# The low part of a pair's queries in six banks behind the last six blocks of key features

## What is computed

```python
q, k, v = heads(xn @ Wq), heads(xn @ Wk), heads(xn @ Wv)        # 16 heads of 64, 1250 rows
q_prime = relu(q @ proj)                                         # proj is 64 x 256
k_prime = relu(k @ proj)
kv   = einsum('bhsf,bhsd->bhfd', k_prime, v)
attn = einsum('bhsf,bhfd->bhsd', q_prime, kv)
norm = einsum('bhsf,bhf->bhs', q_prime, k_prime.sum(axis=2))
attn = attn / (norm + EPS);  mix = attn @ Wo + bo
```

## Time and profile before

| | |
|---|---|
| median of 3 runs | 1439.13 us (1438.02 to 1443.07) |
| the profiled execution | 1438.47 us |
| its span, first to last instruction | 1436.8 us |
| PE busy | 1378.5 us (96%), 7434 matmuls |
| weight loads (PEld) busy | 1261.5 us (88%) |
| DVE busy | 876.0 us (61%) |
| ACT busy | 534.5 us (37%) |
| POOL busy | 171.3 us (12%) |
| mean granted clock of PE | 0.991 |

### The profile page before, as it was taken

The page is one execution under the profiler, slowest core; times in us unless marked ns, Lnnn a source line. Parts: engine busy times, 40 slices in busy tenths (PEclk is TensorE's granted clock), DMA queues, the critical chain, the costliest instruction groups (busy, mean ns, idle before and its releaser), DMA issues.

```text
span 1436.8 us, 19199 instructions
## 1 busy us (share of the span) xinstructions
PE 1378.5 (96%) x7434; PEld 1261.5 (88%) x7434; DVE 876.0 (61%) x1604; ACT 534.5 (37%) x629; POOL 171.3 (12%) x169
## 2 busy tenths in 40 slices
PE   6999999999999999899999999999999989999995
PEld 5888889999999999899999999999978868888884
DVE  6555668787887787645766522445566785544423
ACT  4333244444453543414222223432211225554533
POOL 0011211101101001000000000000000343322212
PEclk9999999999999999999999999999999989999998
DMA  9765432432432433948454014222185665988764
GB/s 311 234 170 128 89 54 32 101 79 36 91 88 34 85 73 56 349 127 220 128 143 120 20 55 127 84 86 69 59 219 172 165 223 158 294 224 232 197 175 73
DMA packets 108573, 193.22 MB, mean 134 GB/s; under 512 B 32289, under 2 KB 77337, under 8 KB 106764
## 3 DMA queue, kind: packets, MB, share of 16 engines
q1 hardware_dynamic: 88563, 145.83, 34.5%
q0 software_dynamic: 19920, 46.17, 16.3%
HBM read 129.38 MB, written 72.21 MB: 140 GB/s over the span
## 4 chain that ended last, share of the span: by engine, by line
PE 71%; DMA 14%; DVE 7%; ACT 3%; issue 2%; SPq 1%; POOLq 0%; ACTq 0%; DVEq 0%
PE slot L2153 23%; PE slot L2311 13%; DMA adj_d<-stage 8%; PE slot L2381 5%; PE slot L2204 5%; PE slot L2212 5%; PE lsb L2212 4%; PE slot L2109 3%; PE kvb L2345 3%; PE slot L2095 2%; PE slot L2084 2%; DMA adj_d<-eye_dram 2%; PE slot L2190 1%; DMA mix_d<-mixn 1%; DMA dx<-x_dram 1%
## 5 line engine op out<-in xcount | busy, mean ns | idle before, releaser
L2153 PE MATMUL slot<-big_hi,slab_h 128*128 128x418 f32 x768 | 193.9, 360 | 9.5 <-DVE qp_l L1755 4.8
L2153 PE MATMUL slot<-big_lo,slab_h 128*128 128x418 f32 x768 | 188.7, 354 | 0.0
L2153 PE MATMUL slot<-big_hi,slab_l 128*128 128x418 f32 x768 | 187.9, 353 | 0.0
L2153 PEld LDWEIGHTS slot<-big_hi,slab_h 128*128 128x128 f32 x768 | 139.2, 189 | 14.4 <-DVE qp_l L1755 6.4
L2153 PEld LDWEIGHTS slot<-big_hi,slab_l 128*128 128x128 f32 x768 | 144.8, 189 | 2.3
L2153 PEld LDWEIGHTS slot<-big_lo,slab_h 128*128 128x128 f32 x768 | 144.7, 189 | 2.1
L1000 POOL DMA_DIRECT2D adj_d<-stage x80 | 67.1, 839 | 483.1 <-ACT stage L1120 364.7
L1393 DVE TENSOR_TENSOR big_lo<-slot,big_hi 128x1024 fp32r<-128x1024 f32 (+2 forms) x70 | 63.2, 928 | 100.2 <-ACT big_hi L1120 100.0
L2311 PE MATMUL slot<-adj,xs_h 125*128 125x418 f32 x480 | 118.1, 354 | 0.5 <-DVE ztmp L1393 0.5
L2311 PE MATMUL slot<-adj,xs_l 125*128 125x418 f32 x480 | 117.4, 353 | 0.0
L1397 DVE TENSOR_SCALAR oh_src<-lane,src_lo 125x125 bf16<-125x125 f16 x320 | 84.0, 263 | 25.5 <-PE kvb L1969 18.3
(11 more groups left out here) (360 smaller groups left out, 2855.2 us busy)
## 6 DMA issues: line engine op xcount, KB each, us to landing
slab_raw<-slabs_dram SPq DMA_DIRECT2D x40, 512.0 KB, 4.2
adj_d<-stage POOLq DMA_DIRECT2D x81, 117.2 KB, 3.1
plain_l<-w_dram SPq DMA_DIRECT2D x16, 512.0 KB, 7.3
w_home<-w_dram SPq DMA_DIRECT2D x8, 1024.0 KB, 5.9
plain_h<-w_dram SPq DMA_DIRECT2D x14, 512.0 KB, 6.2
adj_d<-eye_dram POOLq DMA_DIRECT2D x1, 6250.0 KB, 25.3
raw<-adj_d SPq DMA_DIRECT2D x3, 1828.8 KB
dx<-x_dram SPq DMA_DIRECT2D x10, 448.0 KB
```

Of the source, the lines that this page charges most:

```text
L2153: mm = ten.matmul(ps[:, 512 * q:512 * q + CW], w[a][:, kt, :], big[b][:, kt, CW * q:CW * q + CW], start=(kt == 0 and c == 0), stop=(kt == ...
```

## The change

In ORDER a step QL is put behind each of KK 4 to KK 9, six to a pair: QL (p, h, q) is the low part of bank q (418 columns) of half h, with h = (i - 4) // 3 and q = (i - 4) % 3. The step QE stays where it was, but only ACT (high part) and SP act on it; in `DVE_KINDS` QL stands in its place. So the low part of half 0 is made in three subtractions of 64 x 418 behind the low parts of KK 4, 5 and 6, that of half 1 in three behind KK 7, 8 and 9, where one subtraction of 64 x 1254 stood behind KK 4 and one behind KK 7. The waits of PE name the last bank of the half: `free_slot` behind Q waits for ("QL", p, 1, 2), `feature_product` of half 0, block 0 for ("QL", p, 0, 2). Each QL waits for ACT's QE of its half and increments dve_done.

```diff
--- before.py
+++ after.py
@@ -145,6 +145,7 @@
             o += [("EP", last), ("E", last)]
         for i in range(3, NT):
             o += [("KV", p, i - 3), ("KK", p, i)] + {4: [("QE", p, 0)], 7: [("QE", p, 1)]}.get(i, [])
+            o += [("QL", p, (i - 4) // 3, (i - 4) % 3)] if i >= 4 else []
         if not more:
             o += [("KV", p, NT - 3), ("KV", p, NT - 2), ("RH", p - 1), ("QP", p, 0, 0), ("KV", p, NT - 1), ("KC", p),
                   ("QP", p, 0, 1), ("S", p)]
@@ -219,7 +220,7 @@
 PSUM_KINDS = {"DG", "DT", "Z", "H", "HT", "XT", "V", "K", "Q", "KK", "QP", "AT",
               "O", "OT", "N", "FT", "R", "RT", "PX"}
 ACT_KINDS = PSUM_KINDS - {"OT", "PX", "DG", "DT", "Q", "N"} | {"P", "ZP", "KC", "S", "RH", "LNB", "MP", "RP", "QE", "WV", "VL"}
-DVE_KINDS = {"ZP", "Z", "P", "XT", "WV", "VL", "K", "QE", "KK", "S", "QP", "RC", "RH", "OT", "N", "DN", "DT",
+DVE_KINDS = {"ZP", "Z", "P", "XT", "WV", "VL", "K", "QL", "KK", "S", "QP", "RC", "RH", "OT", "N", "DN", "DT",
              "FL", "FT", "RK", "RX", "SL", "MP", "RP"}
 
 
@@ -1725,14 +1726,18 @@
                     dve.wait_ge(act_done, ACTED[k])
                     tt(v_cols(v_p[1][:, :, :]), v_cols(v_raw[:, :, :]),
                        v_cols(v_p[0][:, :, :].bitcast(F32)), ALU.subtract).then_inc(dve_done, 1)
-                elif kind in ("K", "QE"):
-                    parts = k_s if kind == "K" else q_s
-                    ps = sums[SLOT[(kind[0], k[1])]]
-                    for h in (0, 1) if kind == "K" else k[2:]:
-                        dve.wait_ge(*((half_made, k[1] + 1) if kind == "K" and h == 0 else (act_done, ACTED[k])))
-                        ins = tt(chunks(parts[h][own[1 - h], :]), cols(ps)[own[h]],
-                                 chunks(parts[h][own[h], :].bitcast(F32)), ALU.subtract)
+                elif kind == "K":
+                    for h in range(2):
+                        dve.wait_ge(*((half_made, k[1] + 1) if h == 0 else (act_done, ACTED[k])))
+                        ins = tt(chunks(k_s[h][own[1 - h], :]), cols(ps)[own[h]],
+                                 chunks(k_s[h][own[h], :].bitcast(F32)), ALU.subtract)
                     ins.then_inc(dve_done, 1)
+                elif kind == "QL":
+                    p, h, q = k[1:]
+                    part = slice(CW * q, CW * q + CW)
+                    dve.wait_ge(act_done, ACTED[("QE", p, h)])
+                    tt(q_s[h][own[1 - h], part], sums[SLOT[("Q", p)]][own[h], 512 * q:512 * q + CW],
+                       q_s[h][own[h], part].bitcast(F32), ALU.subtract).then_inc(dve_done, 1)
                 elif kind == "KK":
                     dve.wait_ge(act_done, ACTED[k])
                     dve.scalar_tensor_tensor(
@@ -1946,7 +1951,7 @@
                     elif before[0] == "DG":
                         ten.wait_ge(deg_ready, 1)
                     elif before[0] == "Q":
-                        ten.wait_ge(dve_done, DVED[("QE", before[1], 1)])
+                        ten.wait_ge(dve_done, DVED[("QL", before[1], 1, 2)])
                     elif before[0] == "AT" and before[2] == 0:
                         ten.wait_ge(act_done, ACTED[before])
                         ten.wait_ge(nrm_low, before[1] + 1)
@@ -2089,7 +2094,7 @@
 
                 p, h, f = k[1:]
                 if h == 0 and f == 0:
-                    ten.wait_ge(dve_done, DVED[("QE", p, 0)])
+                    ten.wait_ge(dve_done, DVED[("QL", p, 0, 2)])
                 for c, part in enumerate((proj_h, proj_l[h])):
                     for q in range(3):
                         mm = ten.matmul(ps[:, 512 * q:512 * q + CW], part[:, 128 * f:128 * f + 128],
```

## The result

The changed kernel takes 1455.31 us (median of 4 runs, 1454.67 to 1458.65), the kernel before 1440.05 us (median of 4, 1438.02 to 1443.07): the ratio is 1.0108, with a 95% interval of 1.0092 to 1.0125. It is 15.3 us slower; 13.0 was forecast. The profiled execution took 1458.65 us, the slowest of the four; its span is 1457.0 us. One execution of experiment 4 took 1528.23 us at a mean granted clock of 0.848 and is left out of that experiment's median and ratio.

A forecast was written before the change was run, and what follows sets the result against it. PE was taken to bound the kernel (71% of the chain of waits), delayed by DVE. Seven pairs at +1.82 us plus 0.3 for the last gave +13.0: 1452.1 us median, 1451.5 profiled; range 1446.0 to 1456.5.

The forecast's parts named there:

- The place of the cost: On PE, QP of half 0, block 0 waits for q's last bank, with KV 8, KV 9 and the next K slab queued behind.
- Duration of a bank, 0.59: On DVE, each 64 x 418 subtraction takes 0.59 us, from a straight line between measured shapes; ends 0.43 and 0.68.
- No overlap around a bank: On DVE, a bank and a neighbouring low part of KK don't overlap: 0.62 and 0.70 us, a round of 1.32.
- rival (a): DVE's rounds are shorter, with overlap ahead of a bank: +1.38 us a pair, 1449.1 us in all; chance 0.18.
- A pair, 1.82: In pairs 0 to 6, PE's first QP starts 1.82 us later per pair, the removed KV 5 stall of 0.59 included.
- The last pair, +0.3: In the last pair, the store of att is issued up to 0.5 us later behind DVE; 0.3 us counted.
- rival (d): PE's new wait of 2.4 us at QP lowers its clock: 17 us more, 1469 us; chance 0.03.
- a granted clock under 1.00 between 185 and 620 us: Sign of a wrong prediction: PE's clock falls below its upper level, 2.4 GHz, in the stretch of the head pairs.
- the priced 2.4: Cost per pair if PE ran at half clock behind its QP wait for a stretch as long as the wait: 2.4 us.
- The sum: Seven pairs at 1.82 us and 0.3 for the last: 13.0 us slower, profile 1451.5, median 1452.1 us; chance 0.66.
- The range: Total time from 1446.0 to 1456.5 us; the long end, 2.36 us a pair, gives 1456.1, plus 0.4 for spread.
- banks of 0.68 us: Long end of a bank's duration on DVE, from the 512 row; without overlap +2.36 us a pair.

The follow-up runs named there:

- experiment 4: Changed kernel with QP of half 0, block 0 moved behind KV 8, KV 9 and KC in pairs 0 to 6: 1445.16 us, ratio 1.0028 to before.
- Experiments 3: Changed kernel without the subtraction of bank 2 of half 1 in pairs 1 to 7, QP waiting for bank 1: 1448.56 us, ratio 1.004 to before.
- experiment 1: Changed kernel with its six bank subtractions at the old places, three behind KK 4 and three behind KK 7: 1441.29 us, ratio 0.9999 to before.
- experiment 5: Changed kernel run again: 1457.14 us, ratio 1.0102 to before; with ten added matmuls in PE's wait at QP in pairs 0 to 6: 1452.03 us.
- experiment 6: Changed kernel with the six banks two row blocks earlier, behind the low parts of KK 2 to KK 7: 1437.87 us, ratio 0.9965 to before.

## Why the prediction was right, and where its sizes were off

- *The place of the cost.* That QP waits for the last bank, and that KV 8, KV 9 and the K slab stand behind it, is what the trace after shows, seven times. Experiments 3 and 4 show it from two sides.
- *Duration of a bank, 0.59.* Measured 0.591 (mean of 48).
- *No overlap around a bank.* Right, and rival (a) falls. By the Trainium skill's page "VectorE: DVE Perf Modes", section "Two Vector instructions with no wait between them", which gives its rule as a model, a move holds itself and the next operation when partition halves change, and a like move behind a like one isn't held. The trace agrees with both halves of it: 0.72 and 0.62 from start to start where the kind changes, 0.50 in experiment 1 where it doesn't.
- *A pair, 1.82.* Measured 2.04. Two terms were small: a low part of KK to a bank is 0.72 from start to start, not 0.70, and a bank to a low part 0.62 to 0.63, not 0.62, so a round is 1.344 instead of 1.32, five times 0.024 = 0.12. And PE's restart behind a wait, 0.10, was left out, though the trace of before held it: KV 5's second matmul started 0.22 behind its first (302.76 and 302.54), the others are 0.12 apart. Over seven pairs the two make 1.5 us.
- *The last pair, +0.3.* Its one mechanism was right and a bit small: the store was issued 0.69 us later behind QP in both profiles, up to 0.5 had been counted. The term itself came out at -0.3 and 0.0, because the store took 12.89 and 13.18 us instead of 13.85. Each is one draw of a transfer whose length varies, so its sign isn't settled.
- *The clock, rival (d), given 0.03.* This step was wrong in kind. One wait of 2.61 us without a loss was taken as cover for seven of 2.35. It happened in two of the seven in the first profile, in none of the seven in the second. The prediction had named a granted clock under 1.00 between 185 and 620 us as a sign of being wrong, and the first profile shows that sign three times. With 1.4 us each its price is small, the priced 2.4 too high, and always paying it too pessimistic.
- *The sum.* The regular part explains 14.0 us (with the -0.3) to 14.3 (with 0.0); the medians differ by 15.3 and, in experiment 5's set, by 14.6. The interval of the first is 13.2 to 18.0 us, so the rest, 0.3 to 1.3, is below what the runs tell apart; a spell in a run would be of that size.
- *The range.* Its upper end, 1456.5, stood on banks of 0.68 us, which didn't occur. What was left out (the restart, the longer rounds, the spells) happened to fit in the room that this gave: 1455.31 lies within it partly by luck. The profiled execution, forecast at 1451.5, took 1458.65.

## What to carry to other kernels

Cutting a long operation to relieve one wait moves its end too: look at who waits for the end, and what is queued behind that waiter, before looking at the stall in the middle. The pieces must begin early enough that the last ends no later than the whole did; here two row blocks turned +1.1% into -0.35%. When an engine's rounds (1.34 us) are longer than those of the engine that it feeds (1.19 us), each further round puts it behind by the difference; here DVE's idle time ahead of the rounds paid for that (experiment 6), and with no idle time left the engine behind it paid.

## What the hardware showed that was not expected

**The clock behind a wait.** Nine profiles (the eight kernels, the changed one twice) have one wait of 2.46 to 2.96 us ahead of pair 0's first KV. In six the granted clock fell to 0.50, between 0.7 us ahead of the wait's end and 1.0 behind it, at 2.62, 2.63, 2.79, 2.81, 2.87 and 2.96 us; in three it didn't, at 2.46, 2.61 and 2.61. At QP's waits of 2.16 to 2.36 us it fell in 3 of 15. None followed the waits of up to 1.0 us in the pairs. The length of one wait doesn't decide it: elsewhere in these profiles it fell behind waits of 1.84, 1.86 and 1.88 us, and not behind one of 2.74 (experiment 6, ended at 63.87) or of 2.21 (PE kept busy, ended at 694.23). So a single row of a wait without a loss, as the earlier trace rows, is one draw and no bound.

**Like moves overlap, unlike ones don't.** Three subtractions that move the same half start 0.50 us apart (0.59 each), while a change between a move and a full-height operation costs 0.12 to 0.13 us against the overlap. Six banks among six low parts of KK have twelve such changes where the two long ones had four, so cutting an operation of this kind costs little while the pieces stay together, and more when others stand between them.
